# Macaron block on one core: three transfers and two pairs of weight fetches earlier in the sync queue, three lo-splits of z later on VectorE

## The reference

```python
x = x + 0.5 * ffn(layernorm(x))       # silu(x Wg^T) * (x Wu^T), then Wd^T; hidden size 2048
x = x + scan(layernorm(x))            # below
x = x + 0.5 * ffn(layernorm(x))       # same weights again

def scan(x):                          # K = 4 decay rates lam = sigmoid(lam_logit)
    z = x @ W.T
    m[t, :, k] = lam[k] * m[t-1, :, k] + z[t]
    h = z + sum_k eta[k] * m[..., k]
    return gamma * (h - mean) * rsqrt(var + 1e-5) + beta
```

## Time and profile before

| | |
|---|---|
| median of 3 runs | 1068.14 us (1067.67 to 1068.19) |
| the profiled execution | 1068.19 us, its span 1066.4 us |
| TensorE busy | 1046.1 us (98%), granted clock 0.99 in the mean |
| VectorE, ScalarE, GpSimd busy | 645.5, 349.8, 109.4 us (61, 33, 10%) |
| moved by the transfers | 218.42 MB, 205 GB/s in the mean |
| `dn` loads, 512 KB each | 112, median 3.3 us from issue to landing |

### The profile page before, as it was taken

The page is one execution under the profiler, slowest core; times in us unless marked ns, Lnnn a source line. Parts: engine busy times, 40 slices in busy tenths (PEclk is TensorE's granted clock), DMA queues, the critical chain, the costliest instruction groups (busy, mean ns, idle before and its releaser), DMA issues.

```text
span 1066.4 us, 12736 instructions
## 1 busy us (share of the span) xinstructions
PE 1046.1 (98%) x4704; PEld 864.6 (81%) x4704; DVE 645.5 (61%) x970; ACT 349.8 (33%) x579; POOL 109.4 (10%) x127
## 2 busy tenths in 40 slices
PE   6799999999999999999999999999999999999998
PEld 5688888888888888888888888888888888888886
DVE  7656575567577657877667775687666333323342
ACT  4545444425222222222523222222333322222311
POOL 4223333100020010001002001000000000000000
PEclk7899999999999999999999999999999999999999
DMA  5498877676456555556546555565566566556264
GB/s 177 161 355 291 332 275 274 246 285 231 157 193 208 175 182 186 188 183 210 171 138 210 189 182 178 189 199 182 181 217 207 198 200 199 183 183 204 85 222 165
DMA packets 56333, 218.42 MB, mean 205 GB/s; under 512 B 5840, under 2 KB 14032, under 8 KB 48080
## 3 DMA queue, kind: packets, MB, share of 16 engines
q1 hardware_dynamic: 56128, 217.60, 59.7%
q10 hardware_dynamic: 144, 0.00, 0.0%
HBM read 173.54 MB, written 44.04 MB: 204 GB/s over the span
## 4 chain that ended last, share of the span: by engine, by line
PE 95%; DVE 3%; DMA 1%; issue 0%; POOL 0%; DVEq 0%; ACT 0%; SPq 0%; POOLq 0%; ACTq 0%
PE ps_a L1116 8%; PE ps_a L1118 8%; PE ps_a L1117 8%; PE ps_b L1118 7%; PE ps_b L1116 7%; PE ps_b L1117 7%; PE ps_d L1116 6%; PE ps_d L1118 6%; PE ps_c L1116 6%; PE ps_c L1118 6%; PE ps_d L1117 6%; PE ps_c L1117 6%; PE aux L1118 3%; PE aux L1116 3%; PE aux L1117 3%; PE ps_d L1268 1%
## 5 line engine op out<-in xcount | busy, mean ns | idle before, releaser
L715 DVE TENSOR_TENSOR tmp<-tmp,ps_c 128x512 f32<-128x512 f32 x60 | 41.3, 688 | 148.8 <-PE ps_c L1118 148.8
L1116 PE MATMUL ps_a<-xt,gu 128*128 128x512 f32 x312 | 123.7, 396 | 2.1 <-DVE xt L804 2.1
L1118 PE MATMUL ps_a<-xt,gu 128*128 128x512 f32 x312 | 122.3, 392 | 0.0
L1117 PE MATMUL ps_a<-xt,gu 128*128 128x512 f32 x312 | 122.2, 392 | 0.0
L1116 PE MATMUL ps_b<-xt,gu 128*128 128x512 f32 x288 | 112.8, 392 | 0.0
L1117 PE MATMUL ps_b<-xt,gu 128*128 128x512 f32 x288 | 112.2, 390 | 0.0
L1118 PE MATMUL ps_b<-xt,gu 128*128 128x512 f32 x288 | 112.2, 389 | 0.0
L1116 PE MATMUL ps_d<-dn,hid 128*128 128x512 f32 x256 | 100.8, 394 | 0.0
L1118 PE MATMUL ps_d<-dn,hid 128*128 128x512 f32 x256 | 99.8, 390 | 0.0
L1117 PE MATMUL ps_d<-dn,hid 128*128 128x512 f32 x256 | 99.7, 389 | 0.0
L1116 PE MATMUL ps_c<-xt,gu 128*128 128x512 f32 x240 | 93.6, 390 | 0.0
(11 more groups left out here) (160 smaller groups left out, 2013.7 us busy)
## 6 DMA issues: line engine op xcount, KB each, us to landing
dn<-dn_kept SPq DMA_DIRECT2D x112, 512.0 KB, 3.3
gu<-gu_kept SPq DMA_DIRECT2D x48, 1024.0 KB, 5.1
gu<-gu_kept SPq DMA_DIRECT2D x48, 768.0 KB, 5.3
gu_kept<-gu SPq DMA_DIRECT2D x16, 1024.0 KB, 4.7
gu_kept<-gu SPq DMA_DIRECT2D x16, 768.0 KB, 4.2
dn_kept<-dn SPq DMA_DIRECT2D x16, 512.0 KB, 5.1
zw<-zw_kept SPq DMA_DIRECT2D x16, 512.0 KB, 3.2
h_t<-w_ffn_in SPq DMA_DIRECT2D x16, 256.0 KB, 4.8
```

Source lines behind the costliest of these rows:

```text
L715: dve.tensor_tensor(dst, u3s(si), p5_bank(si)[:, :], ALU.add).then_inc(c22_done, 1)
L1116: pe.matmul(dst, a_hi, b_hi, start=start, stop=False, skip_group_check=chained)
L1117: pe.matmul(dst, a_hi, b_lo, start=False, stop=False, skip_group_check=chained)
L1118: return pe.matmul(dst, a_lo, b_hi, start=False, stop=stop, skip_group_check=chained)
```

## The change

On the sync queue, between the end of stage 0's sets and the loads for `down1`: `fetch_zw(0)` and the load of gamma come directly behind the last load of `x`, ahead of `fetch_a(16)`; the load of beta, `fetch_a(17)` and `fetch_b(17)` come behind `keep_dn(15)`, ahead of `fetch_dn(17)`. Before, these five stood among `fetch_dn(19)` to `fetch_dn(28)`. On VectorE, in stages 1 and 2: `lo_z` of v = 5, 6, 7 is taken out of `before_c12` in sets 6, 7, 8 and put into `before_c11` in sets 7, 8, 9.

```diff
             sp.dma_start(x_tok[:, 12:16, :], x_v[3]).then_inc(x_late[1], 16)
+            sp.wait_ge(zw_stored, 16 * DT)
+            fetch_zw(0)
+            sp.wait_ge(dn_lo, HT - 1)
+            sp.dma_start(gamma, gamma_in.rearrange("(o d) -> o d", o=1).to_broadcast([P, D])
+                         ).then_inc(gamma_arrived, 16)
             sp.wait_ge(gua_stored[0], 16 * 8)
             fetch_a(16)
             sp.wait_ge(gub_stored[0], 16 * 8)
...
             sp.wait_ge(dn_stored[1], 16 * 5)
             fetch_dn(16)
             keep_dn(15)
+            sp.wait_ge(dn_lo, HT)
+            sp.dma_start(beta, beta_in.rearrange("(o d) -> o d", o=1).to_broadcast([P, D])
+                         ).then_inc(beta_arrived, 16)
+            sp.wait_ge(gua_stored[1], 16 * 8)
+            fetch_a(17)
+            sp.wait_ge(gub_stored[1], 16 * 8)
+            fetch_b(17)
             sp.wait_ge(dn_stored[2], 16 * 5)
             fetch_dn(17)
             sp.wait_ge(dn_stored[0], 16 * 6)
             for n in range(18, 35):
                 fetch_dn(n)
-                if n == 19:
-                    sp.wait_ge(gua_stored[1], 16 * 8)
-                    fetch_a(17)
-                if n == 22:
-                    sp.wait_ge(gub_stored[1], 16 * 8)
-                    fetch_b(17)
-                if n == 25:
-                    sp.dma_start(gamma, gamma_in.rearrange("(o d) -> o d", o=1).to_broadcast([P, D])
-                                 ).then_inc(gamma_arrived, 16)
-                    sp.dma_start(beta, beta_in.rearrange("(o d) -> o d", o=1).to_broadcast([P, D])
-                                 ).then_inc(beta_arrived, 16)
-                if n == 28:
-                    sp.wait_ge(zw_stored, 16 * DT)
-                    fetch_zw(0)
...
                     if si == 2:
                         stats_z(p, 2)
                         stats_z(p, 3)
+                    if 7 <= si < 10:
+                        lo_z(p, si - 2)
                     if si in (10, 15):
...
                     if si == 5:
                         norm_z(p, 4)
-                    if 6 <= si < 9:
-                        lo_z(p, si - 1)
```

## The result

The changed kernel takes 1075.97 us (median of six runs, 1075.38 to 1078.0), the kernel before beside it 1068.16 us. The ratio, which also counts nine more runs of the changed kernel (fifteen in all, 1075.38 to 1078.07, median 1076.81), is 1.0079, 95% interval 1.0068 to 1.009: slower by 8.4 us, where 4.9 were forecast. By that ratio it would stand at 1076.6 us against the prediction's base, past the upper end of the range. The profiled execution has a span of 1075.3 us against 1066.4.

A forecast was written before the change was run, and what follows sets the result against it. TensorE was taken as the bound, busy 1046.1 of 1066.4 us, so the edit could hardly gain. 1068.19 + 2.8 (`lo_z` moves) + 2.1 (sync queue) = 1073.1 us, range 1070.3 to 1076.0.

The forecast's parts named there:

- Part 1, 2.8 us: `lo_z` moves: free in sets 7 and 9; in set 8 TensorE's transposes wait 1.4 us, at p = 1 and 2.
- the 0.07 that I had added: Set 8's transposes: 0.07 us for semaphore and row refill, on top of 1.33 us of lateness.
- Part 2: Sync queue: `dn` 17 lands at 233.6, so `down1` at m = 1 starts 2.0 us late, 2.1 with restart.
- rival (a): Sync queue: `dn` 17 isn't held up, so only the `lo_z` moves cost, 1071.0 us; chance 0.17.
- That swallows them: Queue ahead of `dn` 16: 2 us of idle time hide zw and gamma, 786 KB or 1.9 us; cost 0.
- The 2.4 us of slack: `dn` 16: landed at 226.4, needed at 228.84, slack said to cover zw and gamma even without the idle queue.
- a seventh of these bytes is a store, so I take 400: Queue from 222.29 through `dn` 17: 3.67 MB at 400 GB/s take 9.2 us.
- the upper bound: `dn` 17 at 360 GB/s: lands at 234.6, cost 3.1 us with the restart.
- all else: Landing of `dn` 17: 2.1 us of a lone transfer's 3.4 us that aren't its bytes.
- rival (c): TensorE's clock falls after a stall, 1.7 us each: one fall gives 1074.8 us, three 1078.2; chance 0.12.
- the forecast stall of 2.1 us: TensorE at `down1` m = 1, waiting for `dn` 17: 2.0 us plus restart.

The follow-up runs named there:

- lo_z_57: The kernel before with the `lo_z` moves of v = 5 and 7 only, v = 6 left in its place: 1067.41 us, ratio 1.0001.
- dn18_waits: All sync-queue moves of the change, but the queue issues `dn` 18 only once `dn` 17 has landed: 1073.45 us, ratio 1.0056.
- lo_z_only: The kernel before with the VectorE `lo_z` moves only, the sync queue unchanged: 1070.01 us, ratio 1.0024.
- back_no_beta: The kernel before with only `fetch_a(17)` and `fetch_b(17)` moved ahead of `fetch_dn(17)`: 1070.07 us, ratio 1.0027.
- plain_load: back_no_beta plus a plain 262 KB load from 128 places where beta's load had been moved to: 1072.44 us, ratio 1.0052.
- dn17_first: All sync-queue moves of the change, but `fetch_a(17)` and `fetch_b(17)` stand behind `fetch_dn(17)`, ahead of `dn` 18: 1071.49 us, ratio 1.0034.
- zw_no_beta: back_no_beta plus the 524 KB load of zw put behind the store of `dn` 15: 1071.77 us, one run.
- back_only: The kernel before with beta, `fetch_a(17)` and `fetch_b(17)` moved ahead of `fetch_dn(17)`, zw and gamma in their old places: 1072.65 us, ratio 1.0052.
- store_twice: back_only plus a second 524 KB store behind that of `dn` 15: 1076.58 us, ratio 1.0088.
- sync_only: The kernel before with all sync-queue moves of the change and no `lo_z` move: 1073.51 us, ratio 1.0056.
- store_twice_no_beta: back_no_beta plus a second 524 KB store behind that of `dn` 15: 1074.45 us, one run.
- zw_behind: back_only plus the 524 KB load of zw put behind the store of `dn` 15: 1075.72 us, ratio 1.0077.

## Why the prediction went wrong, and where it was right

**Part 1, 2.8 us: right.** Right were which of the three places costs, why (`lo0` behind ScalarE behind `prod1`), and the size: 0.24% (0.15 to 0.33) or 2.6 us measured alone. That the other four moves are free was shown by `lo_z_57`. The hand-over from VectorE to TensorE was 0.15 us, twice the 0.07 that I had added.

**Part 2, place and mechanism: right; size: 2.0 us forecast, 4.6 measured.** A transfer lands behind what was issued before it, and the bytes ahead of `dn` 17 made it late; rival (a) is gone. Two steps of the sum failed, and a third term was put at nothing.

First, "That swallows them": the front was costed at 0, and it cost 1.2 us once the back was there. The row of 221 to 223 us was read as 2 us of idle queue ahead of `dn` 16, but `dn` 16 is issued at 222.29, so 0.7 us of it lie behind the issue. Two more windows of the kernel before:

```profile
220.00:221.00 1.00, 1.00 (x6) 0.84 (x5) 1.00 (x3) 0.00 (x0) 0.00 (x0) 1.00 0.77 320
221.00:222.00 1.00, 1.00 (x6) 0.84 (x5) 1.00 (x3) 0.00 (x0) 0.00 (x0) 1.00 0.05 18
```

The queue stopped near 220.8, some 1.5 us ahead of the issue, and 786 KB need 1.9 us at 414 GB/s, more if the broadcast of gamma is as dear as that of beta, which no run shows apart. About 0.5 MB was left over. The 2.4 us of slack covered `dn` 16 (it landed after 5.6 us, at 228.0, needed at 228.93), but not `dn` 17, which stands behind in the same queue.

Second, "a seventh of these bytes is a store, so I take 400": `dn18_waits` has 351 GB/s in the mean. Two prices stand behind that. A second store of 524 KB costs 1.95 us and not the 1.3 of its bytes; if the first one costs the same, that is 0.7 us more, of which 400 instead of 414 GB/s had set 0.3 aside. The 262 KB of beta were taken as bytes, 0.65 us; the broadcast costs 1.25, 0.6 us more, and makes its neighbours dearer.

1.2 + 0.7 - 0.3 + 0.6 = 2.2 of the 2.6 us; the other 0.4 are about what such a difference can be off by. The rate of 360 GB/s for the upper bound was nearly the one measured. What broke the bound were the bytes: 4.2 MB instead of 3.67 at 360 GB/s are 11.7 us, which gives 236.1 for `dn` 17 and 4.5 us of stall. The 2.1 us of "all else" held.

**Third, the clock.** The sum had it at nothing, as rival (c) with a chance of 0.12, and it came true in the profiled execution, for 2.07 us with the restart where I had 1.7. The mis-sized stall made it likelier, but even the forecast stall of 2.1 us wasn't safe: one of 2.17 us had the fall. The clock of TensorE behind each stall, by the granted clock of the rows: at 1.3 us (`lo_z_only`) it stayed at 1.00; at 2.17 (`back_no_beta`) it fell to 0.50; at 2.28 (`plain_load`) it stayed; at 2.62 (`dn17_first`), 3.36 (`zw_no_beta`) it fell; at 3.42 (`back_only`) it stayed; from 4.12 us on it fell in each of six kernels. Between 2.2 and 3.4 us it went either way, in one execution each. From the restart to m = 3 it took 8.32 us in the changed kernel and 6.39 in `back_only`, whose clock stayed, so the fall by itself cost 1.9 us; in `store_twice` it was 8.99, 2.6 us. It may also be why the medians of `plain_load` and `back_only` lie above their profiled executions (1070.12 and 1071.84 us, the lowest of their runs). The mean clocks of their other runs are 0.988 to 0.992, against 0.991 and 0.992; that fits a fall in some of them, but the kernel before varies from 0.990 to 0.995 by itself, so it isn't shown.

The page "TensorE: Matmul & The Clock Gate" of the Trainium skill, section "HAM oscillation — how this bites in real kernels", ties the fall to longer gaps than 2.17 us; the runs here show falls after gaps as short as that, so the measurement decides. Of the page "DMA: Bandwidth & Descriptors", section "Queues, rings and completion order", I had taken that descriptors of one ring are taken in order: the runs agree, as the 1.2 us for 524 KB more of load ahead and the move of the stall in `dn17_first` show. Its section "Two DMAs through the same engine are not ordered" says that nothing orders transfers across the 16 engines; the lone busy engine in `dn18_waits` is in line with that, in so far as the engines don't finish together.

**Near the end** 0.8 us came back, since the two waits for `dn` there shrank from 1.0 to 0.2 us. That is no gain of the change: over the profiled executions of all these kernels they came to anything from 0 to 1.1 us, and `sync_only`, with the same queue, had 1.1. Why they vary no run shows.

The sum with the measured terms: 1068.19 + 2.6 (part 1 alone) + 4.6 + 2.0 (clock) - 0.8 = 1076.6, against 1076.0, the median of the six runs, and 1076.8, that of all fifteen.

## What to carry to other kernels

A transfer moved ahead of one with a deadline costs that one its own time in the queue, and in these runs this was its bytes only for plain loads: a store cost half as much again and a broadcast of one row twice its bytes. Don't let a gap of just the right size swallow anything, and measure it up to the issue of the next transfer; what is left over is paid by every transfer behind, not only by the next one. A split or copy moved "one operation later" is free or costs more than its own length, depending on what its engine must still wait for in between; find the slowest wait in the new order, not the idle time of the engine. On a kernel whose matmuls run without a gap, a stall of over 2 us may cost 1.5 to 2.5 more through the clock.

## What the runs showed of the hardware that I had not expected

- A broadcast of one row of 2 KB to 128 partitions: the 16 engines fully busy at 277 GB/s over 3 us, 416 to 429 GB/s without it, and 1.25 us of queue time for 262 KB; the plain load of that size 0.1 us (low for its bytes, within the scatter of 0.3).
- A store of 524 KB took 1.95 us of queue time, a load of 524 KB 1.2 us, both in the same place.
- After a stall of TensorE of 2.17 us at the full clock, out of a long stretch of closed work, the granted clock was 0.50; after one of 3.42 us it was 1.00.
- How long TensorE runs at the lower clock behind its restart doesn't follow the length of the stall. By windows of 0.2 us it was 4.8 us behind a stall of 4.12 us (`store_twice_no_beta`), 3.4 behind 4.61 (`sync_only`), 4.2 behind 4.69 (the changed kernel), 4.0 behind 5.27 (`zw_behind`) and 5.6 behind 6.45 (`store_twice`).
